# Flamingo attention and mixture-of-experts layer on one core: the row maxima of the softmax turned by VectorE's 32x32 block transposition instead of TensorE

## The chip, the cores and the metric

One core of a Trainium2 chip runs the whole program in one launch. The metric is the device time of a run in microseconds (us). Engine names are those of the profile: PE is TensorE's matmul side and PEld its weight loads, DVE is VectorE, ACT is ScalarE, POOL is GpSimd, SP is SyncE, whose queue issues the transfers (DMAs).

## The reference, cut to what matters

```python
x = x + tanh(g_xattn) * attention(layernorm(x), ctx, ctx)   # x: 64 x 128 x 512, ctx: 64 x 128 x 128
x = x + tanh(g_ffn) * moe(layernorm(x))                     # 32 experts, top 4, capacity 64, and a shared FFN

# attention: 32 query heads, 8 key heads (one key head serves 4 query heads), head size 16
scores = einsum('bkgsd,bktd->bkgst', qh, kh) / sqrt(16)
weights = softmax(scores, axis=-1)
out = einsum('bkgst,bktd->bkgsd', weights, vh)
```

The mixture of experts is untouched by the change and fills the second stage of the program. The change lies in the attention stage.

## The kernel before

**Stages.** The first stage (747.96 us of the span) goes over 64 batches of 128 tokens: layer norm, attention, residual, second layer norm, router, choice of the experts. The second stage holds the shared and the routed FFN. The change touches the first stage alone.

**One batch.** The 8 key heads are handled as four pairs, which the code calls `c` = 0 to 3; I call the work of one pair's turn a slot. Each pair has 2 x 4 query heads. The scores are computed twice. The first pass (`p_max`, L701, queries on the partitions) serves only to find each query's largest score; VectorE reduces it to `negmax`, the negative maximum, one number for each query and head (L559). The second pass (`p_exp`, L660) has the keys on the partitions, so the maximum can't be a per-partition bias there. It is instead one row of the matmul's operand: `qt` holds the queries transposed, its rows 0 and 64 (one for each of the two key heads) hold the negative maxima, and `kt` holds ones in those rows. ScalarE then takes the exponential (L438).

**How the maxima get into that row.** TensorE transposes `negmax` (128 x 8) into `p_mt` (8 x 128, L709), ScalarE copies that to `mt` (L461), and SP issues two DMAs for each pair (L265), each from four partitions of `mt` to one row of `qt`. TensorE waits for them (`mrow_in`) ahead of the second pass.

**Software pipeline.** Every engine runs its own instruction stream. A turn of the loop, `body(B)`, does the first pass of batch B and the second pass of batch B-1, slot by slot; outputs, second norm and router follow for B-2 to B-4. Two bodies make one turn of the hardware loop; I call them a pair of bodies. One of the two also loads (SP, L297) and splits (ACT L464, POOL L400) a slice of the shared FFN's weights. TensorE's order within a slot is: second pass of the old batch, then extras (values, output transposes, router or key columns), query columns of the next pair (`p_tq`, L620), first pass (L701), transposition of the previous pair's maxima (L709).

**Others that matter.** On GpSimd, one batch's sorting of the expert choice (`top` L385 to `chosen` L395, begun by VectorE's `is_top`, L595) comes ahead of the next batch's key stacks (`ks`, L341 to L344) and query stacks (`qs`, L360, L364) in program order. The query stacks feed `p_tq` of the fourth slot. The load of a later batch's `kv` (L251) waits on SP for `ks_done`, because it overwrites the buffer that the key stacks read; everything behind it on SP's queue waits too. SP's order within a body is: for slot 0 the maxima's row of the previous batch's last pair, `xres`, `xn_rows`; for slot 1 a maxima's row, `xs`, `kv`, `vals`, `xn_cols`; for slot 2 a maxima's row and `out`; for slot 3 a maxima's row; and the weights in one body of two.

Of the kernel before, what the change touches and what calls it, by code (L numbers as in the profile page):

```python
# [14 lines left out]
F32 = mybir.dt.float32  # L15
F32R = mybir.dt.float32r
# [8 lines left out]
G = NH // NKV  # L25
# [73 lines left out]
def build(nc, x, ctx_in, g_xattn, g_ffn, Wr, Wg, Wu, Wd, Wsg, Wsu, Wsd, Wse, out):  # L99
# [7 lines left out]
    with stack:  # L107
# [29 lines left out]
        with ExitStack() as scope:  # L137
# [15 lines left out]
            xn = [sb(f"xn_{i}", [128, E]) for i in range(2)]  # L153
            xnT = [sb(f"xnT{i}", [128, KC, 128]) for i in range(2)]
            wr = sb("wr", [128, KC, NE + 1])
            negmax = [sb(f"negmax{i}", [128, 8]) for i in range(2)]
            mt = [sb(f"mt{i}", [8, 128], F32R) for i in range(2)]
            st1, st2 = sb("st1", [128, 6]), sb("st2", [128, 6])
            mv1 = [sb(f"mv1_{i}", [128, 2]) for i in range(2)]
            mv2 = [sb(f"mv2_{i}", [128, 2]) for i in range(2)]  # L160
# [18 lines left out]
            p_tq = ps("p_tq", [128, 512])  # L179
            p_pv = ps("p_pv", [128, 512])  # L180
            p_ot = ps("p_ot", [128, 512])
            p_mt = ps("p_mt", [8, 128])

            x_in = [sem(f"x_in{i}") for i in range(2)]
            kv_in = [sem(f"kv_in{i}") for i in range(2)]
# [14 lines left out]
            ks_done, qs_done, xn_done = sem("ks_done"), sem("qs_done"), sem("xn_done")  # L200
            pool_chain, dve_chain = sem("pool_chain"), sem("dve_chain")
            tq_mm, k_mm, p1_mm, p2_mm = sem("tq_mm"), sem("k_mm"), sem("p1_mm"), sem("p2_mm")
            pv_mm, ot_mm, mt_mm = sem("pv_mm"), sem("ot_mm"), sem("mt_mm")
            xnT_mm, lg_mm = sem("xnT_mm"), sem("lg_mm")
            max_done, exp_done, tq_done = sem("max_done"), sem("exp_done"), sem("tq_done")
            kt_done, pv_done, mt_done = sem("kt_done"), sem("pv_done"), sem("mt_done")
            ot_done, x2_done, xnT_done, lg_done = sem("ot_done"), sem("x2_done"), sem("xnT_done"), sem("lg_done")

            FIRST, LAST = 5, 61

            def iterations(eng, body, count=None):
                for b in range(FIRST):
# [27 lines left out]
            def _(sp):  # L240
# [12 lines left out]
                def body(B):  # L253
# [2 lines left out]
                        load_in(B + 1)  # L256
                        load_in(B + 2)
                    for c in range(NC):
                        m = (B - 1, 3) if c == 0 else (B, c - 1)
                        if m[0].ok:  # L260

                            b, cc = m
                            wait(sp, mt_done, 4 * b.n + cc + 1)
                            for g2 in range(2):
                                sp.dma_start(qt[b.par][64 * g2:64 * g2 + 1, cc, :].bitcast(F32),  # L265
                                             mt[cc % 2][4 * g2:4 * g2 + 4, :].bitcast(F32)).then_inc(mrow_in[cc % 2], 16)
                        if c == 0:
                            if (B - 1).ok:
                                wait(sp, x2_done, (B - 1).n - 1)
                                sp.dma_start(xres[(B - 1).par][:, :], x_t[(B - 1).n]).then_inc(xres_in[(B - 1).par], 16)  # L270
                            if (B - 3).ok:
                                b = B - 3
                                wait(sp, xn_done, b.n + 1)
                                sp.dma_start(xn_dram[bass.ts(b.n, 128), 0:E], xn[b.par][:, :]).then_inc(xn_out[b.par], 16)
                        if c == 1:
                            if (B + 3).ok:
                                load_in(B + 3)
                            if B.ok:
                                wait(sp, pv_mm, 2 * (B.n - 1))
                                if isinstance(B.n, int) and B.n < 2:  # L280
                                    sp.wait_ge(pads, 4)
                                sp.dma_start(vals[B.par][:, :, 0:D], ctx_in[B.n].rearrange("t (g d) -> t g d", d=D)).then_inc(v_in[B.par], 16)
                            if (B - 3).ok:
                                b = B - 3
                                wait(sp, xnT_done, b.n + 1)
                                alone(sp, spare_s)
                                sp.dma_start(xT_dram[:, :, bass.ts(b.n, 128)].rearrange("k p t -> p k t"), xnT[b.par][:, :, :]).then_inc(xnT_out[b.par], 16)
                        if c == 2 and (B - 2).ok:
                            b = B - 2
                            wait(sp, x2_done, b.n + 1)  # L290
                            sp.dma_start(out_rows[bass.ts(b.n, 128), :], x2[b.par][:, :]).then_inc(x2_out[b.par], 16)
# [114 lines left out]
            def _(act):  # L406
# [22 lines left out]
                def body(B):  # L429
# [3 lines left out]
                    for c in range(NC):  # L433
# [19 lines left out]
                            q_evac(B, c + 1)  # L453
                        if c == 3 and (B + 1).ok:
                            q_evac(B + 1, 0)
                        b, cc = (B - 1, 3) if c == 0 else (B, c - 1)
                        if b.ok:

                            act.wait_ge(mt_mm, 4 * b.n + cc + 1)
                            wait(act, mrow_in[cc % 2], 32 * (2 * b.n + cc // 2))  # L460
                            nc.scalar.activation(mt[cc % 2][:, :], p_mt[:, :], ACT.Copy).then_inc(mt_done, 1)  # L461
                    if weights_split(B):
                        act.wait_ge(wst_in, 32 * (B.pair + 1))
                        nc.scalar.activation(w_cols(wgu_h, B.pair), wst_cols, ACT.Copy).then_inc(whi_done, 1)  # L464
# [3 lines left out]
            def _(dve):  # L468
# [6 lines left out]
                    nc.vector.memset(qs[i][:, :, :, :, 0:16], 0.0).then_inc(pads, 1)  # L475
                nc.vector.memset(kt[0][:, :, :].bitcast(F32), 0.0)
                nc.vector.memset(kt[1][:, :, :].bitcast(F32), 0.0).then_inc(pads, 1)
                nc.vector.memset(ks[:, :, 0:16], 0.0).then_inc(dve_chain, 1)
                chain = Count(dve_chain)
                chain.at = 1  # L480
# [47 lines left out]
                def body(B):  # L528
# [4 lines left out]
                    for c in range(NC):  # L533
# [21 lines left out]
                            x2_stats = stats(x2[B.par][:, :], st2)  # L555
                        if B.ok:
                            dve.wait_ge(p1_mm, 4 * B.n + c + 1)
                            wait(dve, mt_mm, 4 * B.n + c - 1)
                            nc.vector.tensor_reduce(negmax[c % 2][:, :].rearrange("p (g i) -> p i g", i=G),  # L559
                                                    p_max[:, :, :].rearrange("p a (h g t) -> p (a h) g t", g=2, t=128),  # L560
                                                    AX.X, ALU.max, negate=True).then_inc(max_done, 1)
                        if c == 0:
                            if (B + 1).ok:
                                norm_x(B + 1)
                            if (B + 2).ok:
                                x_stats = stats_x(B + 2)
# [34 lines left out]
            def _(pe):  # L601
# [47 lines left out]
                def body(B):  # L649
# [3 lines left out]
                    for c in range(NC):  # L653
                        b = B - 1
                        if b.ok:

                            pe.wait_ge(mrow_in[c % 2], 32 * (2 * b.n + c // 2 + 1))
                            wait(pe, exp_done, 4 * b.n + c)
                            for g2 in range(2):
                                last = mm(p_exp[:, g2, :], kt[b.par][:, c, 128 * g2:128 * g2 + 128], qt[b.par][:, c, :],  # L660
                                          start=True, stop=True)
                            last.then_inc(p2_mm, 1)
# [32 lines left out]
                        if B.ok:  # L695
# [5 lines left out]
                                last = mm(p_max[:, i // 2, 256 * (i % 2):256 * (i % 2) + 256], qt[B.par][:, c, 128 * i:128 * i + 128],  # L701
                                          kt[B.par][:, c, :], start=True, stop=True)
                            last.then_inc(p1_mm, 1)
                        b, cc = (B - 1, 3) if c == 0 else (B, c - 1)
                        if b.ok:

                            pe.wait_ge(max_done, 4 * b.n + cc + 1)
                            wait(pe, mt_done, 4 * b.n + cc)
                            last = tr(p_mt[:, :], negmax[cc % 2][:, :], ident[:, :])  # L709
                            last.then_inc(mt_mm, 1)  # L710
                iterations(pe, body)


# [497 lines left out]
```

## Time and profile before

| what | value |
|---|---|
| time, median of 3 runs | 2355.34 us (2355.14 to 2355.68) |
| the profiled execution's own time | 2355.15 us |
| its span | 2353.3 us |
| first stage | 747.96 us |
| busy over the span: PE / DVE / ACT / POOL | 98% / 48% / 34% / 25% |
| busy from 100 to 200 us: PE / DVE / ACT / POOL | 98.87 / 88.93 / 87.98 / 68.11 us of 100 |
| granted TensorE clock in the first 700 us | 1.00 |

The span's shares are a mean over two stages with different limits; for this change only the stretch up to 748 us counts. A matmul's end is modelled in the trace, so PE's busy time is an upper bound of its real work.

### The profile page before, as it was taken

What the parts mean: (1) busy time and instruction counts of PE and PEld (TensorE: products, weight loads), DVE (VectorE), ACT (ScalarE), POOL (GpSimd) and SP (SyncE); (2) the same over time, 40 slices, a digit from 0 to 9 for tenths busy, and PEclk for the clock granted to TensorE, in tenths of its full rate; (3) what the DMA queues carried; (4) which work ended last, traced back from release to release, by engine and by line L of the source; (5) the groups of instructions that cost most, each with busy time, mean ns of one, the idle gap of its engine ahead of it and who ended that gap; (6) DMA issues with size and microseconds to landing.
All of it is one profiled execution on the core that took longest, in us unless ns stands there. A gap on an engine that the chain in (4) does not pass through costs nothing.

```text
span 2353.3 us, 41796 instructions
## 1 busy us (share of the span) xinstructions
PE 2300.9 (98%) x12545; PEld 1775.7 (75%) x12545; DVE 1137.8 (48%) x2218; ACT 804.6 (34%) x1440; POOL 585.7 (25%) x1395
## 2 busy tenths in 40 slices
PE   7999999999998999999999999999999999999899
PEld 5777777777776877777777777778777787777577
DVE  6888888888886842232323323233222332223132
ACT  6888888888885111010110101011010110101010
POOL 5666666666663100000000000000000000000000
PEclk9999999999998999999999999999999999999899
DMA  3555455455545132222222222223222132223221
GB/s 81 137 145 140 133 142 141 138 136 142 143 131 169 19 116 79 85 96 80 84 78 72 106 80 85 78 64 115 78 87 78 62 115 79 87 78 116 85 72 43
DMA packets 271244, 235.10 MB, mean 100 GB/s; under 512 B 122337, under 2 KB 198113, under 8 KB 271202
## 3 DMA queue, kind: packets, MB, share of 16 engines
q1 hardware_dynamic: 266850, 221.90, 31.4%
q0 software_dynamic: 4352, 12.65, 1.7%
q8 instruction: 25, 0.41, 0.1%
q14 instruction: 17, 0.14, 0.0%
HBM read 161.88 MB, written 71.57 MB: 99 GB/s over the span
## 4 chain that ended last, share of the span: by engine, by line
PE 66%; DVE 1%; DMA 1%; issue 0%; DVEq 0%; POOL 0%; POOLq 0%
PE acc L1117 7%; PE p_u L1133 7%; PE p_u L1135 7%; PE p_u L1134 7%; PE acc L1118 7%; PE acc L1119 7%; PE p_g L1133 7%; PE p_g L1135 7%; PE p_g L1134 7%; PE p_x L1165 2%; PE p_y L1152 2%; PE p_x L1152 2%; PE p_x L1143 0%; DMA out_dram<-eo,cur_tok 0%; DMA rows<-out_dram 0%
## 5 line engine op out<-in xcount | busy, mean ns | idle before, releaser
L1051 DVE TENSOR_TENSOR act_f<-p_u,act_f 128x512 f32<-128x512 f32 x176 | 121.7, 691 | 998.1 <-PE p_u L1135 998.0
L956 ACT ACTIVATE act_f<-p_g 128x512 f32<-128x512 f32 x176 | 105.3, 598 | 1219.1 <-PE p_g L1135 1198.2
L559 DVE TENSOR_REDUCE negmax<-p_max 128x8 f32<-128x1024 f32 x256 | 313.2, 1223 | 80.9 <-PE p_max L701 67.3
L1117 PE MATMUL acc<-wd_h,hh 128*128 128x512 f32 x704 | 280.5, 398 | 0.0
L1133 PE MATMUL p_u<-xh,wgu_h 128*128 128x512 f32 x704 | 274.1, 389 | 4.0 <-DVE act_f L1051 4.0
L1133 PE MATMUL p_g<-xh,wgu_h 128*128 128x512 f32 x704 | 275.6, 391 | 0.0
L1118 PE MATMUL acc<-wd_l,hh 128*128 128x512 f32 x704 | 275.3, 391 | 0.0
L1119 PE MATMUL acc<-wd_h,hl 128*128 128x512 f32 x704 | 275.1, 391 | 0.0
L1135 PE MATMUL p_g<-xh,wgu_l 128*128 128x512 f32 x704 | 274.0, 389 | 0.0
L1135 PE MATMUL p_u<-xh,wgu_l 128*128 128x512 f32 x704 | 273.9, 389 | 0.0
L1134 PE MATMUL p_g<-xl,wgu_h 128*128 128x512 f32 x704 | 273.9, 389 | 0.0
L1134 PE MATMUL p_u<-xl,wgu_h 128*128 128x512 f32 x704 | 273.9, 389 | 0.0
L438 ACT ACTIVATE probs<-p_exp 128x1024 f32<-128x1024 f32 x256 | 260.6, 1018 | 27.8 <-PE p_exp L660 22.0
L921 POOL DMA_INDIRECT out_dram<-eo,cur_tok x32 | 31.2, 974 | 877.0 <-DVE eo L1080 698.6
L701 PE MATMUL p_max<-kt,qt 128*128 128x256 f32 x1024 | 185.4, 303 | 1.8 <-DVE negmax L559 1.8
L660 PE MATMUL p_exp<-qt,kt 128*128 128x512 f32 x512 | 182.4, 437 | 0.2
L620 PEld LDWEIGHTS p_tq<-ident,qs 128*128 128x128 f32 x1024 | 118.9, 147 | 73.3 <-issue 47.1
L620 PE MATMUL p_tq<-ident,qs 128*128 128x128 f32 x1024 | 163.3, 283 | 10.5 <-POOL qs L364 9.6
L422 ACT ACTIVATE qt<-p_tq 128x512 fp32r<-128x512 f32 x256 | 151.5, 592 | 59.6 <-PE p_tq L620 58.0
L1117 PEld LDWEIGHTS acc<-wd_h,hh 128*128 128x128 f32 x704 | 132.7, 188 | 47.8 <-DVE hl L1057 13.0
L1133 PEld LDWEIGHTS p_u<-xh,wgu_h 128*128 128x128 f32 x704 | 132.1, 188 | 32.2 <-DVE act_f L1051 4.8
L1119 PEld LDWEIGHTS acc<-wd_h,hl 128*128 128x128 f32 x704 | 132.7, 189 | 28.3
(142 smaller groups left out, 3581.3 us busy)
## 6 DMA issues: line engine op xcount, KB each, us to landing
ew<-in_L_ffn_Wg_dram SPq DMA_DIRECT2D x32, 704.0 KB, 6.0
ew<-in_L_ffn_Wu_dram SPq DMA_DIRECT2D x32, 704.0 KB, 7.3
xs<-in_x_dram SPq DMA_DIRECT2D x64, 256.0 KB, 2.7
xres<-in_x_dram SPq DMA_DIRECT2D x64, 256.0 KB, 2.8
out_dram<-x SPq DMA_DIRECT2D x64, 256.0 KB, 2.0
xn_rows<-xn SPq DMA_DIRECT2D x64, 256.0 KB, 3.0
xn_cols<-xnT SPq DMA_DIRECT2D x64, 256.0 KB, 2.5
rows<-out_dram SPq DMA_DIRECT2D x16, 1024.0 KB, 5.3
```

Of the source, the lines that this page charges most:

```text
L422: nc.scalar.activation(qt[b.par][:, c, :], p_tq[:, :], ACT.Copy).then_inc(tq_done, 1)
L438: nc.scalar.activation(probs[c][:, :], p_exp[:, :, :].rearrange("p a b -> p (a b)"), ACT.Exp, scale=float(D) ** -0.5).then_inc(exp_done, 1)
L559: nc.vector.tensor_reduce(negmax[c % 2][:, :].rearrange("p (g i) -> p i g", i=G), p_max[:, :, :].rearrange("p a (h g t) -> p (a h) g t", g ...
L620: last = tr(p_tq[:, 128 * i:128 * i + 128], qs[b.par][:, c, i, :, :].rearrange("p g r -> p (g r)"), ident[:, :])
L660: last = mm(p_exp[:, g2, :], kt[b.par][:, c, 128 * g2:128 * g2 + 128], qt[b.par][:, c, :], start=True, stop=True)
L701: last = mm(p_max[:, i // 2, 256 * (i % 2):256 * (i % 2) + 256], qt[B.par][:, c, 128 * i:128 * i + 128], kt[B.par][:, c, :], start=True, s ...
L1117: mm(acc[:, j, :], a[:, t], wd_h[:, f, :], start=(f == 0), stop=False)
L1118: mm(acc[:, j, :], a[:, t], wd_l[:, f, :], start=False, stop=False)
L1119: last = mm(acc[:, j, :], b[:, t], wd_h[:, f, :], start=False, stop=(f == FC - 1))
L1133: mm(bank[:, :], wgu_h[:, w, k, cols], xh[:, k, :], start=(k == 0), stop=False)
L1134: mm(bank[:, :], wgu_h[:, w, k, cols], xl[:, k, :], start=False, stop=False)
L1135: last = mm(bank[:, :], wgu_l[:, w, k, cols], xh[:, k, :], start=False, stop=(k == KC - 1))
```

## The change

The 128 x 8 maxima of two pairs are now collected in one 128 x 32 tile (16 columns used, the other 16 are zero). After the second of the two, VectorE transposes the tile in 32 x 32 blocks into `maxT`. Block q then holds, on partitions 32q to 32q+15, the maxima of queries 32q to 32q+31 for the 16 rows (2 key heads x 2 pairs x 4 query heads). Four DMAs, one for each block, carry 16 x 32 numbers each to the rows 0 and 64 of `qt`, for both pairs at once. TensorE waits for the row once for two pairs. The transposition, the bank `p_mt`, ScalarE's copy `mt` and their semaphores go. There are still eight such DMAs for each batch; they are now issued in two sets of four (at slot 2 for the first two pairs, at slot 0 of the next body for the last two) instead of four sets of two.

```diff
-            negmax = [sb(f"negmax{i}", [128, 8]) for i in range(2)]
-            mt = [sb(f"mt{i}", [8, 128], F32R) for i in range(2)]
+            negmax = [sb(f"negmax{i}", [128, 32]) for i in range(2)]
+            maxT = [sb(f"maxT{i}", [128, 32]) for i in range(2)]
...
-            p_mt = ps("p_mt", [8, 128])
...
+            MROW = 16 * 4
...
@@ SP
-                        m = (B - 1, 3) if c == 0 else (B, c - 1)
-                        if m[0].ok:
-
-                            b, cc = m
-                            wait(sp, mt_done, 4 * b.n + cc + 1)
-                            for g2 in range(2):
-                                sp.dma_start(qt[b.par][64 * g2:64 * g2 + 1, cc, :].bitcast(F32),
-                                             mt[cc % 2][4 * g2:4 * g2 + 4, :].bitcast(F32)).then_inc(mrow_in[cc % 2], 16)
+                        b, h = (B - 1, 1) if c == 0 else (B, 0)
+                        if c % 2 == 0 and b.ok:
+
+                            wait(sp, maxT_done, 2 * b.n + h + 1)
+                            row = qt[b.par][0:65:64, 2 * h:2 * h + 2, :].bitcast(F32).rearrange("p c (i s) -> p (c i) s", i=G)
+                            for q in range(4):
+                                sp.dma_start(row[:, :, 32 * q:32 * q + 32], maxT[h][32 * q:32 * q + 16, :]).then_inc(mrow_in[h], 16)
...
@@ ACT
-                        b, cc = (B - 1, 3) if c == 0 else (B, c - 1)
-                        if b.ok:
-
-                            act.wait_ge(mt_mm, 4 * b.n + cc + 1)
-                            wait(act, mrow_in[cc % 2], 32 * (2 * b.n + cc // 2))
-                            nc.scalar.activation(mt[cc % 2][:, :], p_mt[:, :], ACT.Copy).then_inc(mt_done, 1)
...
@@ DVE
                             dve.wait_ge(p1_mm, 4 * B.n + c + 1)
-                            wait(dve, mt_mm, 4 * B.n + c - 1)
-                            nc.vector.tensor_reduce(negmax[c % 2][:, :].rearrange("p (g i) -> p i g", i=G),
+                            if c % 2 == 0:
+                                wait(dve, maxT_done, 2 * (B.n - 1) + c // 2 + 1)
+                            nc.vector.tensor_reduce(negmax[c // 2][:, 0:16].rearrange("p (g c i) -> p c i g", g=2, c=2)[:, c % 2, :, :].bitcast(F32R),
                                                     p_max[:, :, :].rearrange("p a (h g t) -> p (a h) g t", g=2, t=128),
                                                     AX.X, ALU.max, negate=True).then_inc(max_done, 1)
+                            if c % 2 == 1:
+
+                                dve.wait_ge(max_done, 4 * B.n + c + 1)
+                                wait(dve, mrow_in[c // 2], MROW * B.n)
+                                nc.vector.transpose(maxT[c // 2][:, :], negmax[c // 2][:, :]).then_inc(maxT_done, 1)
...
@@ PE
-                            pe.wait_ge(mrow_in[c % 2], 32 * (2 * b.n + c // 2 + 1))
+                            if c % 2 == 0:
+                                pe.wait_ge(mrow_in[c // 2], MROW * (b.n + 1))
...
-                        b, cc = (B - 1, 3) if c == 0 else (B, c - 1)
-                        if b.ok:
-
-                            pe.wait_ge(max_done, 4 * b.n + cc + 1)
-                            wait(pe, mt_done, 4 * b.n + cc)
-                            last = tr(p_mt[:, :], negmax[cc % 2][:, :], ident[:, :])
-                            last.then_inc(mt_mm, 1)
```

SP's queue in the first of the two bodies of the hardware loop, before: from slot 1's set of the maxima's rows (two DMAs for pair 0) to slot 0 of the next body (register and wait rows between the DMAs are not shown; the numbers in names are buffers):

```order
L265 DMA qt1<-mt0 1x4x128 x2
L249 DMA xs0<-in_x_dram 128x512
L251 DMA kv0<-in_ctx_512_dram 128x128
L282 DMA vals1<-in_ctx_512_dram 128x8x16
L287 DMA xn_cols<-xnT0 128x4x128
L265 DMA qt1<-mt1 1x4x128 x2
L291 DMA out_0_dram<-x2_1 128x512
L265 DMA qt1<-mt0 1x4x128 x2
```

The same stretch of SP's queue now, up to the last two pairs' set at the start of the next body:

```order
L249 DMA xs0<-in_x_dram 128x512
L251 DMA kv0<-in_ctx_512_dram 128x128
L281 DMA vals1<-in_ctx_512_dram 128x8x16
L286 DMA xn_cols<-xnT0 128x4x128
L265 DMA qt1<-maxT0 2x8x32 x4
L290 DMA out_0_dram<-x2_1 128x512
L296 DMA wst<-in_L0_ffn_Wsg_dram 128x4x44
L296 DMA wst<-in_L0_ffn_Wsu_dram 128x4x44
L265 DMA qt1<-maxT1 2x8x32 x4
```

The set ahead of `xs` and the one behind `out` are gone; the rows of the first two pairs stand as four DMAs behind `kv`, `vals` and `xn_cols`, and those of the last two as four DMAs at the start of the next body.

VectorE's stream around the reduction of the fourth slot, before:

```order
L559 TENSOR_REDUCE negmax<-p_max 128x4x2
L583 CAST idx_f<-i 128x4
L516 RECIPROCAL rec<-p_ot 128x16
L526 TENSOR_TENSOR o_sb<-p_ot,rec 128x4x4x16
L503 TENSOR_SCALAR xn<-x_1,mv_1,rs 128x512
L595 TENSOR_TENSOR is_top<-iota_e,idx_f 128x128
```

and now:

```order
L555 TENSOR_REDUCE negmax<-p_max 128x4x2
L562 STREAM_TRANSPOSE maxT<-negmax 128x32
L584 CAST idx_f<-i 128x4
L511 RECIPROCAL rec<-p_ot 128x16
L521 TENSOR_TENSOR o_sb<-p_ot,rec 128x4x4x16
L498 TENSOR_SCALAR xn<-x_1,mv_1,rs 128x512
L596 TENSOR_TENSOR is_top<-iota_e,idx_f 128x128
```

One transposition has come between the reduction and everything that follows it; another stands in the same way behind the second slot's reduction.

## Rows read from the trace of the kernel before

**Rows 1.** Waits from 100 to 700 us: engine, line, releaser, total, times, longest
```profile
POOL top L385 <- DVE is_top L595: 123.9, 54, 2.6
DVE negmax L559 <- PE p_max L701: 47.0, 55, 1.1
PE p_tq L620 <- POOL qs L364: 7.3, 26, 0.3
```

**Rows 2.** Two neighbouring bodies: busy us (and instructions) of each engine
```profile
400.00:411.39 11.39, 11.11 (x86) 8.08 (x85) 9.86 (x22) 10.12 (x20) 7.76 (x20) 1.00 0.49 137
411.39:422.30 10.91, 10.91 (x86) 8.16 (x85) 9.93 (x22) 9.52 (x17) 7.41 (x20) 1.00 0.55 147
```

**Rows 3.** Timeline of VectorE: start us, us, instruction, idle before it
```profile
400.00 1.23 DVE L559 TENSOR_REDUCE negmax<-p_max 128x8 f32<-128x1024 f32 x1 [0.62 <-PE p_max L701]
401.14 0.16 DVE L583 CAST idx_f<-i 128x4 f32<-128x4 uint32 x1
402.29 0.28 DVE L595 TENSOR_TENSOR is_top<-iota_e,idx_f 128x128 f32<-128x128 f32 x1
...
411.39 1.23 DVE L559 TENSOR_REDUCE negmax<-p_max 128x8 f32<-128x1024 f32 x1 [1.12 <-PE p_max L701]
...
413.67 0.28 DVE L595 TENSOR_TENSOR is_top<-iota_e,idx_f 128x128 f32<-128x128 f32 x1
...
422.26 1.23 DVE L559 TENSOR_REDUCE negmax<-p_max 128x8 f32<-128x1024 f32 x1 [0.62 <-PE p_max L701]
```

**Rows 4.** Timeline of GpSimd in the same two bodies
```profile
406.21 0.46 POOL L344 TENSOR_TENSOR ks<-kv,ks 128x128 f32<-128x128 f32 x1
...
408.67 1.43 POOL L364 TENSOR_TENSOR qs<-qraw,qs 128x256 f32<-128x256 f32 x2
...
418.61 1.75 POOL L364 TENSOR_TENSOR qs<-qraw,qs 128x256 f32<-128x256 f32 x2
```

**Rows 5.** Timeline of TensorE: second passes of slots 0 and 2, p_tq
```profile
404.82 0.72 PE L660 MATMUL p_exp<-qt,kt 128*128 128x512 f32 x2
...
410.23 0.65 PE L620 MATMUL p_tq<-ident,qs 128*128 128x128 f32 x4 [0.28 <-POOL qs L364]
...
411.21 0.71 PE L660 MATMUL p_exp<-qt,kt 128*128 128x512 f32 x2
...
416.20 0.71 PE L660 MATMUL p_exp<-qt,kt 128*128 128x512 f32 x2
```

**Rows 6.** Timeline of the weight loads around one transposition of the maxima
```profile
402.34 0.08 PEld L709 LDWEIGHTS p_mt<-ident,negmax 128*8 128x8 f32 x1
402.44 0.30 PEld L660 LDWEIGHTS p_exp<-qt,kt 128*128 128x128 f32 x2
```

**Rows 7.** Groups from 100 to 700 us: the operations that go
```profile
L709 PE MATMUL p_mt<-ident,negmax 128*8 128x128 f32 x215 | 58.3, 271 | 0.0
L461 ACT ACTIVATE mt<-p_mt 8x128 fp32r<-8x128 f32 x216 | 55.7, 258 | 0.0
```

**Rows 8.** Timeline of VectorE at the end of the first stage
```profile
744.23 0.19 DVE L545 COPY lg<-p_ot 128x33 f32<-128x33 f32 x1 [1.11 <-POOL two_sum L389]
744.58 0.20 DVE L571 MAX8 v<-lg 128x8 f32<-128x32 f32 x1 [0.15 <-DVE lg L545]
```

**Rows 9.** Timeline of SP's DMA issues: start us, us of the issue
```profile
406.09 1.23 SPq L265 DMA_DIRECT2D qt<-mt  x2
...
408.15 0.35 SPq L251 DMA_DIRECT2D kv<-in_ctx_dram  x1
408.76 0.63 SPq L282 DMA_DIRECT2D vals<-in_ctx_dram  x1
409.65 0.44 SPq L287 DMA_DIRECT2D xn_cols<-xnT  x1
410.21 1.29 SPq L265 DMA_DIRECT2D qt<-mt  x2
```

**Rows 10.** Timeline of SP and of PEld where the second pass waited
```profile
55.25 1.20 SPq L265 DMA_DIRECT2D qt<-mt  x2
...
57.73 0.30 PEld L660 LDWEIGHTS p_exp<-qt,kt 128*128 128x128 f32 x2 [0.36 <-DMA qt<-mt]
```

**Rows 11.** DMA issues from 100 to 700 us: times, KB each, median us from issue to landing
```profile
out_dram<-x SPq DMA_DIRECT2D x55, 256.0 KB, 2.0
...
kv<-in_ctx_dram SPq DMA_DIRECT2D x53, 64.0 KB, 2.3
```

More of the change, by code:

```diff
@@ L202, in build @@
             tq_mm, k_mm, p1_mm, p2_mm = sem("tq_mm"), sem("k_mm"), sem("p1_mm"), sem("p2_mm")
-            pv_mm, ot_mm, mt_mm = sem("pv_mm"), sem("ot_mm"), sem("mt_mm")
+            pv_mm, ot_mm = sem("pv_mm"), sem("ot_mm")
             xnT_mm, lg_mm = sem("xnT_mm"), sem("lg_mm")
             max_done, exp_done, tq_done = sem("max_done"), sem("exp_done"), sem("tq_done")
-            kt_done, pv_done, mt_done = sem("kt_done"), sem("pv_done"), sem("mt_done")
+            kt_done, pv_done, maxT_done = sem("kt_done"), sem("pv_done"), sem("maxT_done")
             ot_done, x2_done, xnT_done, lg_done = sem("ot_done"), sem("x2_done"), sem("xnT_done"), sem("lg_done")
             FIRST, LAST = 5, 61
+            MROW = 16 * 4
             def iterations(eng, body, count=None):
@@ L477, in _ @@
                 nc.vector.memset(kt[1][:, :, :].bitcast(F32), 0.0).then_inc(pads, 1)
+                nc.vector.memset(negmax[0][:, :], 0.0)
+                nc.vector.memset(negmax[1][:, :], 0.0)
                 nc.vector.memset(ks[:, :, 0:16], 0.0).then_inc(dve_chain, 1)
```

## The prediction

> **What bounds the kernel now.** I read the page first, then the waits and windows of the first stage, then the timelines of two neighbouring bodies, engine by engine. The second stage doesn't contain an instruction of the change, so all of the question is how fast a body of the first stage goes round.
>
> Two bodies take 422.26 - 400.00 = 22.26 us, counted from one fourth-slot reduction to the one after the next [rows 3]. The first takes 11.39 us, the second 10.87. In both PE is busy all but 0.28 us [rows 2], and nothing on it waits long [rows 1]: TensorE is the bound of the second body. The 0.28 us of the first body are a wait of the query columns `p_tq` for GpSimd's query stacks [rows 5], which comes in every second body, 26 times in 600 us [rows 1]. Follow it back: the reduction of slot 3 starts at 400.00, VectorE works through without a gap to the end of `is_top` at 402.57 [rows 3], GpSimd, which idled for that (most of its idle time, [rows 1]), works on to the end of the query stacks at 410.10 [rows 4], `p_tq` starts at 410.23 [rows 5], and the next fourth reduction at 411.39. That is a closed chain through three engines, as long as the first body, and there is no slack in it. In the second body the same chain would need only: 2.56 (reduction start to end of `is_top`, [rows 3]), 6.41 (to the end of the query stacks at 420.36, [rows 4]), 1.29 (from there to the reduction, as in the first body), in sum 10.26 against the 10.87 it takes. The reader is to see that VectorE, busy 9.86 of 11.39 us [rows 2], is on a bounding chain wherever work is put ahead of `is_top`.
>
> **What goes.** The transposition of the maxima (L709) and ScalarE's copy (L461). The matmul's 271 ns [rows 7] is latency and not what PE loses: its weight load starts 0.10 us before the next one [rows 6], and I take 0.10 us of PE for each, four for a body, 0.8 us for a pair of bodies. Bounds: 0.08 (its own weight load) and 0.27 each. ScalarE's copy is 258 ns [rows 7], four for a body, 1.0 us of its 9.5 to 10.1 us [rows 2]. I count it at nothing: ScalarE isn't on the chain above, and PE's work covers it.
>
> **What comes on VectorE.** A 128x32 transposition, twice a body. The trace has none. Nearest by shape are the 128x33 copy and the maximum over 32 columns, 0.19 and 0.20 us [rows 8]; bounds 0.16 (the 128x4 cast, [rows 3]) and 0.28 (the 128x128 `is_top`). It reads what the reduction right before it wrote, and waits for it. Where VectorE waits for its own last result it stands for 0.15 us [rows 8], while instructions without such a wait start some 0.09 us before their predecessor's end: the reduction ends at 401.23, the cast starts at 401.14 [rows 3]. So what follows starts 0.15 + 0.19 us behind the reduction's end instead of 0.09 before it, and loses perhaps 0.07 again by overlap behind the transposition: I take 0.36 us for each. Behind the transposition of slot 3 stand `is_top` and with it the whole GpSimd chain; behind that of slot 1 stands the residual, with slack.
>
> A page of the Trainium skill disagrees with one term: "VectorE: DVE Perf Modes", section "The DRAIN you can't avoid", says that a semaphore between dependent VectorE operations costs nothing extra. By it each transposition would cost about its own 0.19 us; the result is the faster rival below. The trace's 0.15 us gap behind a copy with a dependent operation speaks against it.
>
> **What the row's way costs now.** Per set SP issues four DMAs of 2x8x32. An issue of the old row DMA takes 0.62 us start to start (1.23 and 1.29 for two, [rows 9]); plain 128-row loads take 0.35, `vals` with its short pieces 0.63 [rows 9]. The new pattern is no plainer than the old, so 0.62; bounds 0.35 and 0.65. The fourth starts 3 x 0.62 = 1.86 us behind the first. From an issue's start to the release of TensorE: the trace shows one such wait, where the second of a pair that began at 55.25, so at 55.85, released the second pass at 57.73: 1.88 us [rows 10]. I take that for the low end too, since nothing lands faster [rows 11]; high end 2.3, `kv`. [...] So a set needs 1.86 + 1.88 = 3.74 us from its first issue.
>
> *The last two pairs' set* is ready 0.34 us behind the fourth reduction (at 412.62, start 411.39 + 1.23), with 0.03 for SP: 412.62 + 0.37 + 3.74 = 416.73. The second pass of slot 2 stands at 416.20 [rows 5]: 0.5 us late, likewise in the other body (401.23 + 4.11 = 405.34 against 404.82). Before, that pass had its row from a DMA of its own.
>
> *The first two pairs' set* is worse off, by SP's order. It stands behind `kv`, `vals` and `xn_cols`, and `kv` waits for the key stacks, which in the first body end at 406.67 [rows 4]; before, SP came to `kv` only at 408.15, so this wait cost nothing. Now: key stacks done at 406.67 + 0.36 (transposition ahead of `is_top`) = 407.03; `kv` issued at 407.09; from `kv` to the first row DMA 410.21 - 408.15 = 2.06 us [rows 9]: 409.15; landed at 409.15 + 3.74 = 412.89. The second pass of slot 0 stands at 411.21 [rows 5]: 1.68 us late. Behind it on TensorE stands everything. From there to the next fourth-slot reduction TensorE needs 422.26 - 411.21 = 11.05, less three transpositions of 0.10: 10.75. Sum: 412.89 + 10.75 = 423.64 instead of 422.26. The chain starts and ends at the same reduction of a pair of bodies, so it sets the pace if it is the longest: 1.38 us more for each pair. The stall hides the last two pairs' lateness in the next slot 2, and the other body's first set (its key stacks end without the weights' split before them, about 1.3 us sooner against the pace) comes nearly in time.
>
> 700 us of steady stage are 31 pairs: 31 x 1.38 = 43 us. Made against the profiled execution's 2355.15 us: 2398 us. The median is 0.2 us above that execution, so nothing is to be added.
>
> **The rivals.**
> *The row's latency alone bounds.* If SP reaches the first set in time (the wait for the key stacks doesn't bite, or issues take nearer 0.35 us), the chain is reduction, transposition, 4.11 us, slot 2's second pass, next fourth reduction: 4.11 + 7.80 (404.82 to 412.62) - 0.10 and 4.11 + 7.29 (416.20 to 422.26 + 1.23) - 0.10, less the 0.28 us that the old wait already cost: 22.83 for a pair, 0.57 more, 18 us: 2373. For it: SP's spacing between different DMAs holds gaps of 0.2 to 0.3 us that could shrink. Against it: it needs some 0.8 us less than I count.
> *Rows in time, GpSimd's chain bounds: no change.* 11.39 + 0.36 and 10.26 + 0.36 make 22.37, 0.11 more than now, 3 us: 2358. What TensorE saves then goes into longer waits for the query stacks. It needs the first set 1.7 us sooner, about the whole of three issues.
> *Faster.* One mechanism, the price of the transposition in front of `is_top`. With rows in time, the pair falls below 22.26 once a transposition costs less than (22.26 - 21.65) / 2 = 0.30 us; at 0.19 it is 22.03, 7 us less: 2348. TensorE's own bound, 22.26 - 0.28 - 0.8 = 21.18, would allow 33 us, but GpSimd's chain is in the way.
>
> **How the numbers follow.** First chain 0.62, latency alone 0.17, no change 0.11, faster 0.10. A measurement of this kernel tells about 0.2%, 4.7 us, from no change. So slower 0.79, same 0.11, faster 0.10. The likeliest case's own range is 2385 to 2414: its low end an issue of 0.48 us, half way to the plain load (3 x 0.14 x 31 = 13), its high end a landing of 2.3 us (0.42 x 31 = 13) with issues of 0.65 (0.09 x 31 = 3). The 8-in-10 range goes down to the case of no change, 2357 to 2414, and leaves out the faster case and a little above.
>
> **What would show it.** In the changed kernel's waits the second pass should stand for the DMA `qt<-maxT`, some 1.3 to 1.7 us in slot 0 of every second body, and the wait of `p_tq` for `qs` should go. SP's `kv` should start right behind the key stacks. The transposition should be about 0.19 us with a 0.15 us gap ahead of it; a pair of bodies should take 23.6 us. I am wrong if the row's DMAs issue in 0.35 us, if they land well under 1.9 us, or if SP doesn't reach `kv` before the key stacks end.

## The result and the profile after

The changed kernel takes 2405.22 us (2402.48 to 2406.65, 4 runs) against 2355.44 us (2355.14 to 2355.68, 4 runs): 49.8 us slower, ratio 1.0211 [1.0198, 1.0224]. The profiled execution took 2406.65 us, its span is 2404.8 us, 51.5 us more than before. The first stage ends at 798.44 us instead of 747.96, so 50.5 us of the difference lie there.

What the engines waited for from 100 to 700 us, total us, times and longest; it answers to [rows 1]:

```profile
POOL top L384 <- DVE is_top L596: 125.8, 50, 2.7
DVE negmax L555 <- PE p_max L703: 64.1, 75, 2.3
PE p_tq L621 <- POOL qs L363: 24.0, 25, 1.0
PEld p_exp L662 <- DMA qt<-maxT: 23.3, 24, 1.0
PE p_exp L662 <- DMA qt<-maxT: 19.1, 25, 0.8
PE p_max L703 <- DVE negmax L555: 3.5, 16, 0.6
```

Once in each pair of bodies TensorE now waits for the query stacks, in the fourth slot (25 times), and right behind that, in slot 0 of the next body, for the row (25 times). In [rows 1] the wait for the stacks was there at up to 0.28 us, the wait for the row not at all.

Two neighbouring bodies by windows (columns as in [rows 2]):

```profile
402.86:414.89 12.03, 10.96 (x80) 7.66 (x80) 10.31 (x23) 9.74 (x15) 8.29 (x20) 1.00 0.40 115
414.89:426.67 11.78, 10.98 (x81) 7.98 (x82) 10.37 (x24) 8.60 (x13) 7.45 (x20) 1.00 0.60 146
```

This pair takes 23.81 us, 1.55 more than before; the mean from 100 to 700 us is 23.92. PE idles 1.07 us in the first body and 0.80 in the second; VectorE's busy time rose by about half a microsecond for each body. The clock is the full 2.4 GHz level in both, as before.

VectorE's timeline from the fourth-slot reduction to `is_top`, and the normalisation of the next `x`, which answers to [rows 3]:

```profile
402.86 1.23 DVE L555 TENSOR_REDUCE negmax<-p_max 128x8 fp32r<-128x1024 f32 x1 [0.38 <-PE p_max L703]
404.12 0.21 DVE L562 STREAM_TRANSPOSE maxT<-negmax 128x32 f32<-128x32 f32 x1
404.34 0.17 DVE L584 CAST idx_f<-i 128x4 f32<-128x4 uint32 x1
...
405.50 0.28 DVE L596 TENSOR_TENSOR is_top<-iota_e,idx_f 128x128 f32<-128x128 f32 x1
...
406.84 0.53 DVE L498 TENSOR_SCALAR qraw<-xs,mv,rs 128x512 f32<-128x512 f32 x1
```

The transposition starts 0.03 us behind the reduction's end (402.86 + 1.23 = 404.09) and takes 0.21 us. `is_top` ends 2.92 us behind the reduction's start instead of 2.57. GpSimd's timeline behind it, first in this body and then in the next (it answers to [rows 4]):

```profile
406.43 0.32 POOL L388 TENSOR_TENSOR two_sum<-is_top 128x64 f32<-128x64 f32 x1
406.93 0.56 POOL L391 TENSOR_TENSOR one_sum<-two_sum 128x32 f32<-128x32 f32 x1 [0.18 <-POOL two_sum L388]
...
409.72 0.46 POOL L343 TENSOR_TENSOR ks<-kv,ks 128x128 f32<-128x128 f32 x1
...
412.18 1.41 POOL L363 TENSOR_TENSOR qs<-qraw,qs 128x256 f32<-128x256 f32 x2
...
418.95 0.26 POOL L391 TENSOR_TENSOR one_sum<-two_sum 128x32 f32<-128x32 f32 x1 [0.18 <-POOL two_sum L388]
```

`one_sum`, the same instruction on the same shape, takes 0.56 us in one body and 0.26 in the other. The long one lies beside VectorE's normalisation `qraw` (406.84 to 407.37) and ends right behind it. The key stacks end at 410.18. SP's queue and TensorE behind it (they answer to [rows 9] and [rows 5]):

```profile
410.35 0.35 SPq L251 DMA_DIRECT2D kv<-in_ctx_dram  x1
410.89 0.63 SPq L281 DMA_DIRECT2D vals<-in_ctx_dram  x1
411.77 0.44 SPq L286 DMA_DIRECT2D xn_cols<-xnT  x1
412.36 2.18 SPq L265 DMA_DIRECT2D qt<-maxT  x4
```

```profile
413.73 0.65 PE L621 MATMUL p_tq<-ident,qs 128*128 128x128 f32 x4 [1.04 <-POOL qs L363]
414.13 0.72 PE L703 MATMUL p_max<-kt,qt 128*128 128x256 f32 x4
415.63 0.73 PE L662 MATMUL p_exp<-qt,kt 128*128 128x512 f32 x2 [0.78 <-DMA qt<-maxT]
```

This is one chain. `kv` stood waiting for the key stacks (SP had issued `xs` at 407.98), the row's four DMAs stood behind it, and the second pass behind them. The maxima that they carry had been turned in slot 1, by 410.12. SP's own waits from 100 to 700 us have a line for it, which the kernel before has not:

```profile
SPq L251 <- POOL ks L343: 55.2, 49, 1.9
```

### The profile page after: what moved, and what is told of

Read it like the earlier page. It is cut to its first block, busy times and chain, and to the rows that moved or that the text cites. A ratio compares the mean times of both kernels' runs of the same rounds, so it can differ in the third digit from the quotient of the medians.

```text
span 2404.8 us, 40463 instructions
## 1 busy us (share of the span) xinstructions
PE 2301.9 (96%) x12289; PEld 1759.9 (73%) x12289; DVE 1170.1 (49%) x2348; ACT 765.9 (32%) x1184; POOL 604.1 (25%) x1395
## 4 chain that ended last, share of the span: by engine, by line
PE 65%; DVE 1%; DMA 1%; issue 0%; DVEq 0%; POOL 0%; POOLq 0%
PE acc L1112 7%; PE p_u L1128 7%; PE p_u L1129 7%; PE p_u L1130 7%; PE acc L1113 7%; PE acc L1114 7%; PE p_g L1128 7%; PE p_g L1130 7%; PE p_g L1129 7%; PE p_x L1160 2%; PE p_y L1147 2%; PE p_x L1147 2%; PE p_x L1138 0%; DMA out_dram<-eo,cur_tok 0%; DMA rows<-out_dram 0%
## 5 line engine op out<-in xcount | busy, mean ns | idle before, releaser
L555 DVE TENSOR_REDUCE negmax<-p_max 128x8 fp32r<-128x1024 f32 x256 | 311.9, 1218 | 91.6 <-PE p_max L703 91.6
L662 PE MATMUL p_exp<-qt,kt 128*128 128x512 f32 x512 | 171.1, 415 | 25.2 <-DMA qt<-maxT 25.1
L621 PE MATMUL p_tq<-ident,qs 128*128 128x128 f32 x1024 | 163.6, 283 | 30.1 <-POOL qs L363 29.3
```

The lines of the kernel that those rows point to most:

```text
L555: nc.vector.tensor_reduce(negmax[c // 2][:, 0:16].rearrange("p (g c i) -> p c i g", g=2, c=2)[:, c % 2, :, :].bitcast(F32R), p_max[:, :, : ...
L621: last = tr(p_tq[:, 128 * i:128 * i + 128], qs[b.par][:, c, i, :, :].rearrange("p g r -> p (g r)"), ident[:, :])
```

## The experiments

Each was timed beside the kernel before on the same chip, where that took 2355.4 to 2355.6 us. The experiments ran on three chips, whose medians for the kernel before lie within 0.2 us. "A pair" is the time of two neighbouring bodies, counted between fourth-slot reductions.

**1. The row ahead of the loads.** In the changed kernel the first two pairs' four DMAs go behind `xs` and ahead of `kv`, `vals` and `xn_cols`. All else stays.

```diff
                     sp.dma_start(xs[b.par][:, :], x_t[b.n])...
+                    send_row(B, 0)          # 4 DMAs qt<-maxT, was at slot 2
                     wait(sp, ks_done, b.n - 1)
                     sp.dma_start(kv[b.par][:, :], ctx_in[b.n])...
```

> The changed kernel with one thing moved on SP's queue: the four row DMAs of the first two pairs now stand behind xs and ahead of kv, vals and xn_cols, so they no longer stand behind kv's wait for the key stacks. Three theories. Queue (mine): the set is late because of where it stands; it will start near 2.1 us sooner, land before TensorE comes to slot 0, and the 0.8 to 1.0 us stall there goes. What is left is the GpSimd chain, 12.03 and 10.9 us, or the last two pairs' set: 22.9 us for a pair of bodies instead of 23.81, 2376 us in all. VectorE: the cost is the two transpositions and their waits on a nearly full VectorE; moving DMAs changes nothing, 2400 to 2405 us. Latency: four DMAs one behind the other are late wherever they stand; part of the stall stays, about 2390 us.

2382.85 us (2382.03 to 2384.45), ratio 1.0121 [1.0104, 1.0138]: 22.4 us better than the change. Its waits, 100 to 700 us:

```profile
PE p_tq L627 <- POOL qs L369: 25.5, 26, 1.0
PEld p_exp L668 <- DMA qt<-maxT: 0.4, 1, 0.4
```

The row's wait is gone, so the row's place on SP did cause it. A pair takes 23.11 us, where I had expected 22.9 (2376 us in all); what is left is a wait for the query stacks of 1.0 us in every second body. So the queue is one cause and not the only one.

**2. The key stacks ahead of the sorting.** In the changed kernel GpSimd makes the next key stacks before the sorting, so that they don't wait for `is_top`.

```diff
+                    if (B + 2).ok and not (isinstance(B.n, int) and B.n < 0):
+                        k_stacks(B + 2)
                     b = B - 4
                     if b.ok:
                         pool.wait_ge(top_done, b.n + 1)   # sorting
...
-                        k_stacks(B + 1)
                         q_stacks(B + 1)
```

> The changed kernel with GpSimd's key stacks of the next batch moved ahead of the sorting of the expert choice. kv's wait on SP is then over early, and the query stacks come 1.1 us sooner. Queue theory: SP reaches the first row DMA near 1.9 us sooner, the stall in slot 0 goes, and the wait of the query columns (1.04 us in every second body) goes as well; bound by the last two pairs' row or by VectorE, 22.5 to 22.8 us for a pair, 2363 to 2373 us. VectorE theory: only the chain through the query stacks shortens, by 1.1 us at most where it binds; with VectorE full, 2385 us or more. Latency theory: about 2390 us, with the wait for the row left in slot 0.

2359.82 us (2350.97 to 2361.76, 10 runs), ratio 1.0015 [1.0006, 1.0025]. Both waits go:

```profile
PE p_max L706 <- DVE negmax L558: 10.7, 26, 0.5
PE p_exp L665 <- DMA qt<-maxT: 1.5, 3, 0.5
```

The wait for the stacks doesn't appear at all, and the row's is 1.5 us in 600. A pair takes 22.34 us. One edit in GpSimd's order gives back 45 of the 50 us: SP comes to `kv` with the stacks already made, and the stacks' part of the chain no longer starts at `is_top`. It came out 3 us below the range that I gave it. What stands now is the reduction, late by up to 0.5 us for TensorE's first pass.

**3. Two spare transpositions in the kernel before.** They read and write tiles of their own, stand where the change puts its two, and feed nothing.

```diff
                             nc.vector.tensor_reduce(negmax[c % 2]...)...
+                            if c % 2 == 1:
+                                dve.wait_ge(max_done, 4 * B.n + c + 1)
+                                nc.vector.transpose(spare_out[:, :], spare_in[:, :]).then_inc(turned, 1)
```

> The kernel before with only VectorE's part of the change added: two transpositions of a spare 128x32 tile in each body, each behind a wait for the reduction in front of it, in the same two places; TensorE's transposition, ScalarE's copy and the DMAs as before. Queue theory: the chain through VectorE and GpSimd grows by 0.36 us in each body, but only every second body is bound by it; by rows 22.37 to 22.7 us for a pair, 2359 to 2369 us. VectorE theory: most of the 50 us is here, 2385 us or more.

2381.77 us (2381.09 to 2383.08), ratio 1.0116 [1.0099, 1.0132]: 26.3 us from 0.21 us instructions that nothing needs. VectorE, then GpSimd:

```profile
417.98 0.54 DVE L505 TENSOR_SCALAR qraw<-xs,mv,rs 128x512 f32<-128x512 f32 x1
```

```profile
418.06 0.56 POOL L393 TENSOR_TENSOR one_sum<-two_sum 128x32 f32<-128x32 f32 x1 [0.18 <-POOL two_sum L390]
418.91 0.24 POOL L396 TENSOR_TENSOR chosen<-one_sum,key_of 128x32 f32 x1 [0.28 <-POOL one_sum L393]
```

The bodies take 11.07 and 12.14 us, 0.20 and 0.75 more than before. By the chain of [rows 3] to [rows 5] the long one is 2.98 to the end of `is_top` (+0.41), 4.39 to the end of the key stacks (+0.29), 3.48 to the end of the query stacks and 1.29 to the reduction. The +0.29 is `one_sum`: pushed back by 0.4 us it meets the normalisation (experiment 8 tests this). The transposition of slot 1 doesn't stand on this chain; neither of the two was tried alone. My own expectation, 2359 to 2369, held the shift and not this.

**4. The change without the transposition.** The DMAs read the untransposed `negmax` tile; turning the maxima is left out, so the row's numbers are not the maxima. SP's order and TensorE's work are those of the change.

```diff
-                                nc.vector.transpose(maxT[c // 2][:, :], negmax[c // 2][:, :]).then_inc(maxT_done, 1)
...
-                            wait(sp, maxT_done, 2 * b.n + h + 1)
+                            wait(sp, max_done, 4 * b.n + 2 * h + 2)
```

> The changed kernel without VectorE's transposition: the row DMAs take the same 16x32 pieces straight from the tile of maxima (so the row holds other numbers; the transposing is left out), in the same order on SP behind the same kv. Queue theory: the chain reduction, sorting, key stacks, kv, row, second pass stays and is only 0.36 to 0.65 us shorter, and 0.3 us more where VectorE was full: 22.9 to 23.2 us for a pair, 2375 to 2385 us. VectorE theory: back to 2355 us or below.

2376.35 us (2375.82 to 2377.12), ratio 1.0092 [1.0075, 1.0109], as expected. A pair takes 23.00 us, and the row's wait stands:

```profile
PEld p_exp L657 <- DMA qt<-negmax: 28.3, 27, 1.1
PE p_exp L657 <- DMA qt<-negmax: 23.1, 28, 0.9
```

So SP's order and the sets of four cost 21 us without VectorE's transpositions, what TensorE and ScalarE save already taken off, and the two transpositions 29 us on top of it (2405.22 - 2376.35).

**5. The old transposition, the new sets.** The kernel before, with its two DMAs for each pair of heads gathered into sets of four at the change's places.

```diff
-                        m = (B - 1, 3) if c == 0 else (B, c - 1)
+                        b, h = (B - 1, 1) if c == 0 else (B, 0)
+                        if c % 2 == 0 and b.ok:
+                            wait(sp, mt_done, 4 * b.n + 2 * h + 2)
+                            for cc in (2 * h, 2 * h + 1): ...
```

> The kernel before with only the DMAs' part of the change: TensorE still transposes the maxima and ScalarE still copies them (into four tiles), but SP sends the rows in two sets of four DMAs, at slot 2 behind kv, vals and xn_cols and at slot 0 of the next body. VectorE does nothing more than before. Two chains theory (mine now: the chain VectorE, GpSimd and the chain that leaves it at the key stacks for kv and the row share their first half, each costs some 20 us by itself): like the changed kernel without its transposition, 2371 to 2381 us, with TensorE waiting for the row in slot 0. If the four-DMA sets only hurt together with VectorE's delay: 2355 to 2360 us.

2602.95 us (2593.77 to 2605.28), ratio 1.1052 [1.1033, 1.107]. This missed, and it isn't the clean test that I meant. TensorE turns a pair's maxima one slot after the reduction, so the set's second half is ready a slot later than VectorE's, while the set must land as early as its first half did:

```profile
PE p_exp L660 <- DMA qt<-mt: 125.5, 80, 1.9
```

Twice in each body the second pass waits up to 1.9 us. A smaller part is TensorE's clock: granted 0.97 on average from 100 to 700 us (1.00 in the kernel before), and pairs with a fall in them took up to 32.5 us against 29.3. The run shows that sets of four at these places need maxima that are turned right behind the reduction.

**6. The key stacks ahead of the sorting, in the kernel before.** The edit of experiment 2.

> The kernel before with only GpSimd's key stacks moved ahead of the sorting. If the chain through is_top, sorting, key and query stacks binds every second body of the kernel before, the 0.28 us wait of the query columns goes and that body falls from 11.39 to about 10.9 us: 21.8 us for a pair, 14 us less, 2341 us; if it doesn't bind, 2355 us.

2342.62 us (2341.22 to 2343.40), ratio 0.9942 [0.9925, 0.9958]: 12.8 us faster than the kernel before.

```profile
403.64:414.52 10.88, 10.88 (x86) 8.12 (x85) 10.00 (x21) 9.56 (x18) 7.24 (x20) 1.00 0.54 147
414.52:425.41 10.89, 10.89 (x86) 8.10 (x85) 10.09 (x21) 9.65 (x19) 7.94 (x21) 1.00 0.51 139
```

TensorE is without a gap in both bodies. Against this, its true rival, the change with the same edit (experiment 2) is 17.2 us slower.

**7. Experiments 1 and 2 together.**

> The changed kernel with both repairs: key stacks ahead of the sorting, and the first two pairs' row ahead of kv. With the key stacks early kv no longer waits, so the row's place should matter only by the length of vals and xn_cols, which now come behind it. If VectorE is what binds by then (10.3 us busy and its waits in a body), no change against the key stacks alone, 2355 to 2360 us; if the row still binds, 5 to 10 us less.

2376.26 us (2373.07 to 2378.65), ratio 1.0087 [1.0070, 1.0104]. A miss. SP's queue, then TensorE:

```profile
420.59 0.41 SPq L302 DMA_DIRECT2D wst<-in_L_ffn_Wsg_dram  x1
421.08 0.53 SPq L302 DMA_DIRECT2D wst<-in_L_ffn_Wsu_dram  x1
421.73 2.21 SPq L251 DMA_DIRECT2D qt<-maxT  x4
```

```profile
425.03 0.73 PE L671 MATMUL p_exp<-qt,kt 128*128 128x512 f32 x2 [0.73 <-DMA qt<-maxT]
```

The maxima of the last two pairs were turned at 420.63, but SP had begun the second of the weights' loads at 421.08 and came to the row at 421.73. SP is late because of experiment 1's edit: the first two pairs' set, now ahead of `kv`, waits for its own transposition, which ends at 415.52, and SP stands still behind `xs`. `kv`, `vals`, `xn_cols`, `out` and the weights all come behind it.

```profile
413.38 0.35 SPq L255 DMA_DIRECT2D xs<-in_x_dram  x1
415.55 2.15 SPq L251 DMA_DIRECT2D qt<-maxT  x4
```

In experiment 2, where three of these loads go ahead of the set, SP is through with the weights at 413.43 and waits for the maxima, which are turned at 414.65:

```profile
412.91 0.52 SPq L296 DMA_DIRECT2D wst<-in_L_ffn_Wsu_dram  x1
414.68 2.18 SPq L265 DMA_DIRECT2D qt<-maxT  x4
```

A variant with the weights' loads behind that set wasn't run.

**8. Experiment 3 with the normalisation later.** VectorE's statistics of the next `x` go ahead of the normalisation, which so starts some 0.6 us later. If the normalisation is what holds `one_sum` up, `one_sum` is short again, with the spare transpositions still there. The statistics' tile is doubled for it.

```diff
                         if c == 0:
-                            if (B + 1).ok:
-                                norm_x(B + 1)
                             if (B + 2).ok:
                                 x_stats = stats_x(B + 2)
+                            if (B + 1).ok:
+                                norm_x(B + 1)
```

> The kernel before with two spare transpositions in each body (as measured: 2381.8 us), and VectorE's statistics of x put ahead of its normalisation of x in slot 0, so that the normalisation no longer runs beside GpSimd's one_sum. In that kernel one_sum takes 0.56 us instead of 0.25 and ends when the normalisation ends. If the normalisation keeps GpSimd from the memory, one_sum falls back to 0.25 us and the chain in both bodies is 0.3 us shorter: about 22.6 us for a pair, 2363 us. If not, one_sum stays at 0.56 and the time at 2380 us.

2370.70 us (2370.53 to 2371.47), ratio 1.0062 [1.0046, 1.0079]: 11.1 us better than experiment 3. GpSimd, then VectorE:

```profile
412.74 0.26 POOL L393 TENSOR_TENSOR one_sum<-two_sum 128x32 f32<-128x32 f32 x1 [0.18 <-POOL two_sum L390]
```

```profile
413.25 0.54 DVE L505 TENSOR_SCALAR qraw<-xs,mv,rs 128x512 f32<-128x512 f32 x1
```

`one_sum` is 0.25 or 0.26 us in every body and a pair takes 22.77 us, 0.44 less than in experiment 3. I had expected 0.6 less, and 2363 us. The normalisation now meets other GpSimd instructions: the first of the key stacks takes 0.37 us in one body, the weights' split 1.03 in the other (0.30 and 0.94 in experiment 3). The order of two VectorE instructions changes a GpSimd instruction's length.

**9. No transposition, and the key stacks early.** Experiments 4 and 2 together; turning the maxima is left out here too.

> The changed kernel with key stacks ahead of the sorting and without VectorE's transposition (the row DMAs take pieces of the tile of maxima; the transposing is left out). Tells what binds the changed kernel with key stacks early (2359.8 us). If it is VectorE's time: without 0.4 us in each of two places TensorE binds, whose four removed transpositions are worth 0.8 us for a pair: 21.0 to 21.5 us, 2318 to 2333 us. If it is the sets' way over SP: no lower than 2350 us.

2334.62 us (2333.78 to 2335.37), ratio 0.9912 [0.9895, 0.9928]; a pair takes 21.50 us. That is just above the 2318 to 2333 us that I expected. Two things can be read from it. Against experiment 6, less TensorE and ScalarE work is worth 8.0 us where neither VectorE's transpositions nor GpSimd's chain stand in the way: 0.28 us for a pair and its eight transpositions, where I had counted 0.8. Against experiment 2, VectorE's transpositions cost 25.2 us with GpSimd's chain out of the way; `one_sum`, 0.56 us in every second body there and 0.25 or 0.26 here, is in that.

**10. Room on VectorE.** Experiment 2 with the normalisation of `x` on ScalarE, as one activation with scale and bias; GpSimd makes the bias with two small instructions.

```diff
-                    layer_norm(b, xs, mv1, rs1, rs1_done, qraw, qraw_done)
+                    nc.scalar.activation(qraw[b.par][:, :], xs[b.par][:, :], ACT.Identity,
+                                         bias=nb1[:, 0:1], scale=rs1[:, 0:1]).then_inc(qraw_done, 1)
```

> The changed kernel with key stacks early, and the normalisation of x (0.54 us on VectorE in each body) moved to ScalarE, which the change relieved by 1.0 us a body; GpSimd makes the bias for it in two more small operations. If VectorE binds the changed kernel with key stacks early, this gives back what the transpositions cost there: 21.2 to 21.8 us for a pair, 2325 to 2342 us, at or below the kernel before with key stacks early (2342.6). If the sets' way over SP binds, 2355 us or more; if the two GpSimd operations get into the chain, the same.

2343.93 us (2342.80 to 2344.98), ratio 0.9949 [0.9932, 0.9966]: 15.9 us better than experiment 2, a little above what I expected, and no better than experiment 6. A pair takes 21.81 us. The edit takes VectorE's 0.54 us away and the long `one_sum` with it (0.25 or 0.26 us in every body); how much of the 15.9 us is due to which isn't separated.

**11. The same in the kernel before.** Experiment 6 with the normalisation on ScalarE.

> The control to the last one: the kernel before with key stacks early (2342.6 us) and the normalisation of x moved to ScalarE in the same way. There two bodies take 21.78 us, equal halves, and I hold TensorE for the bound, so relief of VectorE should give nothing: 2339 to 2346 us; and ScalarE, which here still copies the maxima and is busy 88%, could bind: up to 2370 us.

2352.78 us (2351.70 to 2355.32, 10 runs), ratio 0.9989 [0.9980, 0.9999]. The edit that gives 15.9 us in the changed kernel costs 10.2 us here: VectorE wasn't the limit of experiment 6. What the 10.2 us are isn't shown: ScalarE, whose copies of the maxima are still there, is busy 540 of 600 us, and GpSimd has two more instructions. So the relief of VectorE pays in the changed kernel alone.

## Why the prediction was right, and where its terms were off

The forecast was 2398 us, slower, by one chain: fourth reduction, transposition, `is_top`, sorting, key stacks, `kv`, row, second pass, fourth reduction two bodies on. The trace after shows this chain closed, and experiments 1, 2 and 4 take it apart at three places. Its terms, predicted and measured, for a pair of bodies:

| leg | predicted | measured |
|---|---|---|
| reduction's start to key stacks done | 7.03 | 7.32 |
| to `kv`'s issue | 0.06 | 0.17 |
| to the first of the row's DMAs | 2.06 | 2.01 |
| to the second pass | 3.74 | 3.27 |
| to the fourth reduction two bodies on | 10.75 | 11.04 |
| sum | 23.64 | 23.81 |

The mechanism was right. That the sum came within 0.17 us was in part luck: three legs were 0.69 us longer than predicted and two 0.52 us shorter. 31 pairs times 1.55 us make 48 us, but the pair of the table is one of the shorter ones. From 100 to 700 us they take 23.8 or 23.9 us, a single one 25.5 where TensorE's clock fell (granted 0.93 from 528 to 552 us), and with the mean of 23.92 it is 31 x 1.66 = 51 us, against 50.5 between the ends of the first stage.

**The transposition's price.** I took 0.36 us, from an own duration of 0.19 and a wait of 0.15. Measured are 0.21 and 0.03, and the end of `is_top` moves by 0.35 in the change and 0.41 in experiment 3. The sum was right, the split not: the cast starts 0.01 us behind the transposition's end (404.34 and 404.33), so that the 0.07 us that I took off for an overlap never came. On the wait, the Trainium skill ("VectorE: DVE Perf Modes", section "The DRAIN you can't avoid") was nearer than the row I set against it; the faster rival, which I built on it, still fell, since the overlap was lost in its place.

**The sorting.** The +0.29 in the first leg is `one_sum`, 0.56 instead of 0.26 us. I moved the chain by 0.36 us and left each of its instructions at its old length.

**The row's DMAs.** They start at 412.36, 412.97, 413.51 and 414.05, so the fourth 1.69 us behind the first, not 1.86, and it lands 1.58 us behind its start (415.63 - 414.05), not 1.88. "Well under 1.9 us" was one of my signs of being wrong; this term was, the chain was not.

**TensorE's leg.** The three transpositions' 0.30 us didn't come off: 11.04 against 11.05 before. VectorE is the reason. In experiment 4, where it has no transpositions, the same leg is 10.73 us (400.62, a second pass that had waited for the row, to the reduction at 411.35). So "PE saves 0.10 each" held there, and is worth nothing in this kernel: its first pass waits up to 0.6 us for VectorE's reduction instead, 16 times (the last line of the waits after). Over a whole pair 0.10 was too much: the eight transpositions were worth 0.28 us in experiment 9.

**The wait of `p_tq` for the query stacks.** I wrote that it should go. It grew to 1.04 us, since the key and query stacks move back together with `is_top`. The row's wait comes behind it, in slot 0 of the next body, and the last one sets the pace. What I had put at 1.3 to 1.7 us for the row alone is therefore split: 1.04 us for the stacks, then 0.78 for the row. The last two pairs' set, which I put at 0.5 us late, made TensorE wait nowhere, as forecast.

**The rivals.** "Rows in time, GpSimd's chain bounds" was the one most in error: I gave a pair 22.37 us and 3 us in all. Experiments 1 and 3 are this case, and a pair takes 23.11 and 23.21: 26 to 27 us. Of the 0.84 us missing in experiment 3, `one_sum` is 0.6 (0.30 in each body) and the greater shift 0.1; the rest is the query stacks' leg, 3.48 and 3.42 us instead of 3.43 and 3.31. This rival's number was also the low end of the range; the case itself lay well inside. The two halves cost 26 us (experiment 3) and 21 us (experiment 4) alone and 50 together. That this is nearly their sum is in part chance: experiment 3's 26 us come through the query stacks, in both bodies. On the row's chain the transpositions lengthen two legs against experiment 4, from the reduction to the key stacks' end (6.74 us there, 7.32 in the change) and TensorE's (10.73 and 11.04), in sum 0.89 us for a pair or 28 us. "Faster" needed a shift under 0.30 us; it was 0.35 to 0.41.

## What to carry to other kernels

Before work is moved to an engine with a low busy share, follow the chain on which its next instruction stands; here two spare instructions of 0.2 us for each body, one of them ahead of a small `is_top`, were worth 26 us. The work taken off the engine with the highest share brought 8 us in experiment 9 alone, which leaves the turning of the maxima out; no kernel with the whole change was faster than the 2342.6 us of experiment 6. A DMA's place in an in-order queue is a dependence on everything that the queue's earlier entries wait for, and moving it ahead hands its own wait to what stands behind it (experiment 7). And the same order edit belongs in both kernels before they are compared: key stacks ahead of the sorting gives 2342.6 us without the change and 2359.8 with it, and this best version (2342.6) needs none of the change.

## What the runs showed of the hardware

A GpSimd instruction on 128 x 32 numbers (`one_sum`) took 0.26 us alone and 0.56 us where VectorE's 128 x 512 fp32 normalisation from SBUF to SBUF ran, and ended right behind it (407.49 and 407.37; in experiment 3, 418.62 and 418.52); with the normalisation moved (experiment 8) or on ScalarE (experiment 10) it was 0.25 or 0.26 us in every body. The Trainium skill, "SBUF — State Buffer", section "Who interferes with whom", describes this as an exclusive lock of a port pair that the two engines share, in which the later one waits for the whole instruction. The trace agrees as far as `one_sum` goes: it began 0.09 us behind the normalisation and ended 0.12 us behind its end.

The 32 x 32 block transposition of a 128 x 32 fp32 tile takes 0.21 us, and started 0.03 us behind the reduction whose result it reads, where short VectorE instructions that depend on each other stood 0.15 us apart [rows 8].

```profile
L562 DVE STREAM_TRANSPOSE maxT<-negmax 128x32 f32<-128x32 f32 x101 | 21.4, 212 | 8.3
```
